# A tap in eight on GpSimd with partial sums in PSUM, and a reordered last pass, in an fp32 image kernel

## The reference, cut to what matters

```python
# layer 0: 512 channels in 256 groups of two
d = depthwise 3x3 conv, stride 2, padding 1            # (8, 256, 64, 64), 18 taps per output
labels = kmeans(d[0]);  gate = sigmoid(from a mixture fit on cluster means of d)
up = repeat(gate * d + d, 2, axis=1) * w_up
x = bilinear_up_x2(up) + x                             # (8, 512, 128, 128)
# layer 1: attention over 64 low cosine frequencies P (16384 x 64)
xP = einsum('bcn,nk->bck', x, P)                       # then products with Wq, Wk, Wv and norms
out = gamma * (WvxP @ (out / lamdv) + out_bias) + x
```

## Time and profile before

| what | value |
|---|---|
| time, median of 3 runs | 3655.98 us (3652.37 to 3658.43) |
| profiled execution: its own time, its span | 3661.4 us, 3659.6 us |
| TensorE busy in the span, mean granted clock | 85 %, 0.935 |
| VectorE busy | 81 % |
| ScalarE busy | 51 % |
| GpSimd busy | 17 % |
| first pass, start of the first and the last tap (L190) | 18.1 and 1354.6 us |
| second pass, start of the first and the last add | 1941.6 and 3650.4 us |

### The profile page before, as it was taken

The page is one execution under the profiler, slowest core; times in us unless marked ns, Lnnn a source line. Parts: engine busy times, 40 slices in busy tenths (PEclk is TensorE's granted clock), DMA queues, the critical chain, the costliest instruction groups (busy, mean ns, idle before and its releaser), DMA issues. The chain is left out here.

```text
span 3659.6 us, 66212 instructions
## 1 busy us (share of the span) xinstructions
PE 3128.9 (85%) x23398; PEld 2253.8 (62%) x23398; DVE 2957.6 (81%) x3454; ACT 1880.3 (51%) x4327; POOL 637.2 (17%) x325
## 2 busy tenths in 40 slices
PE   7998999999899958995867888889788888888876
PEld 3554545455454526652446877878687787878776
DVE  5999999999999982204556979888897988979877
ACT  4554555555455524241316565655656566565654
POOL 0000000000000000000003333333333333333333
PEclk9999999999999979597978999999999999999999
DMA  6665566556655525252035988988888898888997
GB/s 266 256 248 212 219 257 255 222 212 251 257 233 212 238 114 204 110 217 65 0 132 212 338 331 333 351 317 337 327 326 333 328 347 331 335 326 329 345 346 287
DMA packets 190940, 947.58 MB, mean 259 GB/s; under 512 B 13505, under 2 KB 13633, under 8 KB 170626
## 3 DMA queue, kind: packets, MB, share of 16 engines
q1 hardware_dynamic: 181378, 909.48, 64.3%
q0 software_dynamic: 9216, 33.56, 2.3%
HBM read 638.90 MB, written 301.99 MB: 257 GB/s over the span
## 5 line engine op out<-in xcount | busy, mean ns | idle before, releaser
L190 DVE SCALAR_TENSOR_TENSOR first_acc<-first_x,first_wd,first_acc 128x1024 f32<-128x1024 f32 (+1 forms) x1088 | 1297.9, 1272 | 58.0 <-ACT first_acc L215 45.2
L1290 PE MATMUL second_o<-second_right,second_left 128*128 128x128 f32 x8192 | 1101.0, 285 | 175.2 <-POOL second_left L1074 98.7
L1290 PEld LDWEIGHTS second_o<-second_right,second_left 128*128 128x128 f32 x8192 | 1016.8, 199 | 229.7 <-issue 217.9
L1534 DVE SCALAR_TENSOR_TENSOR second_x<-second_o,second_shift,second_x 128x512 f32<-128x512 f32 x1024 | 732.9, 737 | 233.1 <-PE second_o L1290 231.5
L1074 POOL TENSOR_TENSOR second_left<-second_mid_copy,second_coef_rep 64x1024 f32<-64x1024 f32 x256 | 602.5, 2353 | 1684.5 <-ACT second_mid_copy L1397 1677.4
L219 ACT ACTIVATE first_xT<-first_tp 128x512 f32<-128x512 f32 x1024 | 609.3, 598 | 536.1 <-PE first_tp L245 535.6
L245 PE MATMUL first_tp<-all_const,first_x 128*128 128x128 f32 x4096 | 680.5, 291 | 75.3 <-issue 40.8
L245 PEld LDWEIGHTS first_tp<-all_const,first_x 128*128 128x128 f32 x4096 | 442.3, 143 | 458.7 <-issue 446.3
L257 PE MATMUL first_freq<-first_xT,first_p 128*64 128x256 f32 x4096 | 669.2, 408 | 17.9 <-ACT first_xT L219 8.2
L1376 ACT ACTIVATE second_mid<-second_dd,all_inter 128x128 f32<-128x128 f32 x1024 | 327.1, 390 | 388.1 <-DVE second_mid L1515 384.9
L257 PEld LDWEIGHTS first_freq<-first_xT,first_p 128*64 128x64 f32 x4096 | 210.9, 136 | 194.7 <-issue 178.9
(11 more groups left out here) (233 smaller groups left out, 2005.5 us busy)
## 6 DMA issues: line engine op xcount, KB each, us to landing
second_x<-in_x SPq DMA_DIRECT2D x256, 1024.0 KB, 10.2
out<-second_x SPq DMA_DIRECT2D x256, 1024.0 KB, 6.4
first_x<-in_x SPq DMA_DIRECT2D x48, 4224.0 KB, 25.3
first_x<-in_x SPq DMA_DIRECT2D x16, 4096.0 KB, 14.9
...
downsampled<-first_acc POOLq DMA_DIRECT2D x64, 512.0 KB, 11.5
...
```

The lines of the kernel that those rows point to most:

```text
L190: nc.vector.scalar_tensor_tensor(out=acc[c][:, :, left:], in0=tap_window(xt[c], (s, dh, dw), OUT1), scalar=wd[:, t, k:k + 1], in1=acc[c][: ...
L1290: last = nc.tensor.matmul(ob[n][:, r, :], left[a][:, r, n, :], right[a][:, r, :], start=True, stop=True)
L1534: nc.vector.scalar_tensor_tensor(out=xt[i][:, n // S, n % S, rows, :], in0=ob[n][:, :, :], scalar=shift[:, n:n + 1], in1=xt[i][:, n // S, ...
```

## The change

In the first pass GpSimd takes over 17 taps on the lower half of chunk 3 (`POOL_CHUNK`): an eighth of VectorE's elements. [...] VectorE keeps its running sums in PSUM (`partial`), from tap 2 to tap 16; only its first tap reads `acc` and its last writes it. Chunks 0 and 1 stay as pairs of 1024 elements; in phase 2 it works on three halves of 512. To make room, the transposes have two PSUM buffers in place of four and the fold shares the banks of the sums. Chunk 3's first tap moves on ScalarE from quad 48 to quad 34, stores move to SyncE's queue ahead of each load, and loops hold eight images a turn.

In the last pass `turn_mid` of the next unit goes ahead of the unit's first product, `copy` ahead of both halves of `weight`, `scale_odd` ahead of the first add, `frequencies` behind the fourth, and loads and stores of the two halves `t` have semaphores of their own.

```diff
--- before.py
+++ after.py
-TAPS = [(s, dh, dw) for dw in (0, 1) for dh in (-1, 0, 1) for s in range(S)] + \
-       [(s, dh, -1) for dh in (-1, 0, 1) for s in range(S)]
+TAPS = [(s, dh, dw) for dw in (0, -1, 1) for dh in (-1, 0, 1) for s in range(S)]
 ROWS1 = 32
 CH1 = H // ROWS1
 TAPS_LEFT = len(TAPS) - 1
 OUT1 = ROWS1 // 2
 QUADS = S * ROWS1 // 4
 SLOTS = 4
+TP_BANKS = 2
+UNROLL1 = 4
+POOL_CHUNK = 3
+FIRST_TAPS = [0, QUADS, 2 * QUADS, 2 * QUADS + 2]
+STEPS = [TAPS_LEFT, TAPS_LEFT, 2 * TAPS_LEFT, 2 * TAPS_LEFT]
+
+
+def weight_of(s, dh, dw):
+
+    k = s * 9 + (dh + 1) * 3 + dw + 1
+    return slice(k, k + 1)
...
-        tp = [sc.ps(f"tp{i}", [P, 4, P]) for i in range(SLOTS)]
+        tp = [sc.ps(f"tp{i}", [P, 4, P]) for i in range(TP_BANKS)]
         freq_ps = [sc.ps(f"freq{t}", [P, 512]) for t in range(T)]
-        sum_ps = sc.ps("sum", [P, 512])
+        sum_ps = [bank[:, S * P:S * P + S * UV] for bank in freq_ps]
+        product = sc.sb("product", [P, OUT1 // 2, WD])
+        partial = [sc.ps(f"partial{i}", [P, OUT1, WD]) for i in range(2)]
         halves = sc.sb("halves", [P, S * P])
...
+                def store(i, c):
+
+                    sp.wait_ge(tapped[c], i * STEPS[c] + STEPS[c] + FREE)
+                    if c == POOL_CHUNK:
+                        sp.wait_ge(upper_tapped, i * TAPS_LEFT + TAPS_LEFT + FREE)
+                    sp.dma_start(xd.rearrange("b t g n -> (b t) g n")[i, :, c * OUT1 * WD:(c + 1) * OUT1 * WD],
+                                 acc[c][:, :, :].rearrange("g h w -> g (h w)")).then_inc(stored[c], 16)
+
+                start_free(sp, stored)
+                with sp.Fori(0, B * T - 1) as i:
                     for c in range(CH1):
-                        load(i, c)
+                        store(i, c)
...
+                start_free(pool, [tapped[POOL_CHUNK]])
+                c, rows = POOL_CHUNK, slice(OUT1 // 2, OUT1)
+                for i in range(B * T):
+                    done = i * STEPS[c] + FREE
+                    pool.wait_ge(x_in[c], i * 16 + 16)
+                    pool.wait_ge(started, i * CH1 + c + 1)
+                    for n, (s, dh, dw) in enumerate(TAPS[1:]):
+                        left = 1 if dw < 0 else 0
+
+                        if n > 0 or i > 0:
+                            pool.wait_ge(tapped[c], done + 2 * n)
+                        nc.gpsimd.tensor_scalar(product[:, :, left:],
+                                                tap_window(xt[c], (s, dh, dw), OUT1 // 2, OUT1 // 2),
+                                                wd[:, i % T, weight_of(s, dh, dw)], None, ALU.mult
+                                                ).then_inc(tapped[c], 1)
+                        pool.wait_ge(tapped[c], done + 2 * n + 1)
+                        nc.gpsimd.tensor_tensor(acc[c][:, rows, left:], acc[c][:, rows, left:], product[:, :, left:],
+                                                ALU.add).then_inc(tapped[c], 1)
...
+                def tap(t, c, n, rows, mine):
+
+                    s, dh, dw = TAPS[1 + n]
+                    left = 1 if dw < 0 else 0
+                    row0, count = rows.start, rows.stop - rows.start
+                    before = acc[c] if n == 0 else mine
+                    after = acc[c] if n == TAPS_LEFT - 1 else mine
+                    return nc.vector.scalar_tensor_tensor(
+                        out=after[:, rows, left:], in0=tap_window(xt[c], (s, dh, dw), count, row0),
+                        scalar=wd[:, t, weight_of(s, dh, dw)], in1=before[:, rows, left:],
+                        op0=ALU.mult, op1=ALU.add)
+
+                with dve.Fori(0, B // UNROLL1) as r:
+                    for n_image in range(UNROLL1 * T):
+                        t, i = n_image % T, r * UNROLL1 * T + n_image
+                        for n in range(TAPS_LEFT):
+                            for c in (0, 1):
+                                if n == 0:
+                                    dve.wait_ge(x_in[c], i * 16 + 16)
+                                    dve.wait_ge(started, i * CH1 + c + 1)
+                                    if c == 0:
+
+                                        dve.wait_ge(tapped[2], i * STEPS[2] + FREE)
                                     else:
 
+                                        dve.wait_ge(upper_tapped, i * TAPS_LEFT + FREE)
+                                else:
+
+                                    dve.wait_ge(tapped[c], i * STEPS[c] + n + FREE)
+                                tap(t, c, n, slice(0, OUT1), partial[c]).then_inc(tapped[c], 1)
+                        c, half = 2, OUT1 // 2
+                        for n in range(TAPS_LEFT):
+                            for h in range(2):
+                                if n == 0 and h == 0:
+                                    dve.wait_ge(x_in[c], i * 16 + 16)
+                                    dve.wait_ge(started, i * CH1 + c + 1)
+
+                                    dve.wait_ge(tapped[0], i * STEPS[0] + STEPS[0] + FREE)
+                                elif n > 0:
+
+                                    dve.wait_ge(tapped[c], i * STEPS[c] + 2 * n + h - 1 + FREE)
+                                tap(t, c, n, slice(h * half, (h + 1) * half), partial[0]).then_inc(tapped[c], 1)
+                            if n == 0:
+                                dve.wait_ge(x_in[POOL_CHUNK], i * 16 + 16)
+                                dve.wait_ge(started, i * CH1 + POOL_CHUNK + 1)
+
+                                dve.wait_ge(tapped[1], i * STEPS[1] + STEPS[1] + FREE)
+                            else:
+
+                                dve.wait_ge(upper_tapped, i * TAPS_LEFT + n + FREE)
+                            tap(t, POOL_CHUNK, n, slice(0, half), partial[1]).then_inc(upper_tapped, 1)
...
-                            slot, c = q % SLOTS, q // QUADS
-                            if q % QUADS == 0:
+                            slot = q % SLOTS
+                            if q in FIRST_TAPS:
+                                c = FIRST_TAPS.index(q)
                                 act.wait_ge(x_in[c], i * 16 + 16)
 
-                                act.wait_ge(stored[c], i + FREE)
+                                act.wait_ge(stored[c], i * 16 + FREE)
                                 nc.scalar.activation(acc[c][:, :, :], tap_window(xt[c], TAPS[0], OUT1), ACT.Copy,
...
-                            pe.wait_ge(copied[slot], i * (quads // SLOTS) + q // SLOTS + FREE)
+                            before = (q - TP_BANKS) % SLOTS
+                            pe.wait_ge(copied[before], i * (quads // SLOTS) + (q - TP_BANKS) // SLOTS + 1 + FREE)
...
+                    for t in range(T):
+                        if u % 2 == 1:
+                            store(b, m, t)
+                        if u % 2 == 1 and (more or m + AHEAD < CH2):
+                            load_image(b, m + AHEAD, t)
...
                 def step(b, u, more):
+                    if more or u < UNITS - 1:
+                        turn_mid(b, u + 1)
                     for n in range(BANKS):
                         multiply(b, u, n)
-                        if more or u < UNITS - 1:
-                            if n == 0:
-                                turn_mid(b, u + 1)
-                            elif n == 1:
-                                turn_zt(b, u + 1)
+                        if n == 1 and (more or u < UNITS - 1):
+                            turn_zt(b, u + 1)
                     if more:
                         stage(b + 1, u)
...
-                    ahead = u % 2 == 1 and (more or m + 2 < CH2)
-                    if ahead:
-                        weight(b, m + 2, 0)
                     if more or u < UNITS - 1:
                         copy(b, u + 1)
-                    if ahead:
+                    if u % 2 == 1 and (more or m + 2 < CH2):
+                        weight(b, m + 2, 0)
                         weight(b, m + 2, 1)
...
-                    if n == 0 and u % 2 == 0:
-                        dve.wait_ge(x_in[i], (b * (CH2 // XBUF) + m // XBUF) * T * 16 + T * 16)
+                    if n % S == 0 and u % 2 == 0:
+                        dve.wait_ge(x_in[i][n // S], (b * (CH2 // XBUF) + m // XBUF) * 16 + 16)
...
+                    if more or u < UNITS - 1:
+                        if u == UNITS - 1:
+                            take_coef(b, 1)
+                        scale_odd(b, u + 1)
                     for n in range(BANKS):
                         add(b, u, n)
-                        if n == 0 and (more or u < UNITS - 1):
-                            if u == UNITS - 1:
-                                take_coef(b, 1)
-                            scale_odd(b, u + 1)
-                        if n == 1 and u % 2 == 0 and (more or m + 1 < CH2):
-                            frequencies(b, m + 1)
                         if n == 2 and u % 2 == 0 and (more or m + 1 < CH2):
                             interpolate(b, m + 1)
```

(2 more changed lines are left out.)

101 lines of the change are left out of this document (36 added, 65 removed).

## The result

| | before | changed |
|---|---|---|
| median of 5 runs | 3657.06 us | **3680.87 us** (3670.57 to 3683.67) |
| ratio | | 1.006, 95% interval 1.0042 to 1.0077 |
| profiled execution, span, granted clock | 3659.6 us, 0.935 | 3681.9 us, 0.926 |
| first pass, start of VectorE's last tap | 1354.6 us | 1315.6 us |
| last pass, first to last add | 1941.6 to 3650.4: 1708.8 us | 1898.6 to 3674.8: 1776.2 us |

The kernel became 24 us slower; forecast were 156 faster. The span's +22 us are two changes of opposite sign: the last pass starts 43 us earlier and takes 67 us longer.

The account below looks back on a forecast made before the run. VectorE's work was taken to bound the first pass, with TensorE close behind, and a chain through several engines the last. Profiled 3661.4 - 35 - 100 - 21 = 3505, said as 3500 us against the runs' median; range 3390 to 3600.

Parts of the forecast that it names:

- First pass, -35 us: First pass: image period falls from 82.1 to 79.9 us, over 16 images -35 us.
- A: First pass: PSUM is dear, each VectorE tap takes 0.06 us more, +5 in place of -35, 3540 us; chance 0.12.
- C: First pass: reading and writing the same PSUM bank halves VectorE's rate in the running sums, 4425 us; chance 0.08.
- D: First pass: GpSimd late, its chain takes 82 us, the pass gains nothing, 3535 us; chance 0.06.
- my 0.8 us: First pass: price of one GpSimd product of 512, within a tap of 2.2 us and 37 us an image.
- Last pass, -121 us: Last pass: seven batches with stage gain 100 us, the last batch 21 (205 to 184).
- 11.1 us against 12.68: Last pass: the pair's new chain, from bank 0 of an odd unit, takes 11.1 us where it took 12.68.
- Two banks at 0.9 each: Last pass: first link of the pair's new chain, two TensorE banks at 0.9 us each.
- GpSimd at 2.35: Last pass: link of the pair's new chain behind the copy, GpSimd's half of left at 2.35 us.
- A "new wait" of 1.1, hidden: Last pass: TensorE waits 1.1 us for interpolation, making 10.9 a pair, hidden under 11.1 by little.
- My allowance of 0.4 for DMA: Last pass: a pair taken at 11.5 us, above the chain's 11.1, with DMA needing 11.8 a pair.
- rival B: Last pass: DMA decides earlier, at 345 GB/s a batch's floor is 205 us; 3529 us, or 3560 with waits; chance 0.14.

Follow-up runs that it names:

- e1: Changed first pass with the last pass of the kernel before: 3610.06 us, 0.9881 of the kernel before.
- e11: e1 with VectorE's running sums left in SBUF (acc) from first tap to last: 4056.30 us, 446 us slower than e1.
- e8: Changed kernel with four more TensorE products behind bank 3 of each even unit, ahead of the turn, their result overwritten: 3636.84 us.
- e7: e3 with interpolate behind the second add in place of the third: 3440.32 us, 0.9399 of the kernel before.
- e3: Changed kernel with the first half of the weighting back ahead of the copy: 3486.92 us, 0.9542 of the kernel before.
- e9: e3 with frequencies back behind bank 1, ahead of interpolation: 3603.03 us, 116 us slower than e3.
- e4: Changed kernel with frequencies back behind bank 1, ahead of interpolation: 3809.97 us, 1.0422 of the kernel before.
- e10: e3 with the turn of the middle rows back behind bank 0: 3551.02 us, 64 us slower than e3.
- e2: Changed kernel with the turn of the middle rows (turn_mid) back behind bank 0: 3608.53 us, 0.9883 of the kernel before.

## Why the prediction was wrong, point by point

**First pass, -35 us: right.** The period is 79.9 us, as forecast, with 81.9 and 77.5 in turn; alone it gave 45 us (e1). The cause is the forecast one too, a wait for chunk 3 in every other image, at 3.3 us where my sum had 4.8. Taps at 1.19 and 0.66 held, so rivals A and C did not occur; nor did D, whose 18 us for a single load had no row.

GpSimd's product was mis-sized: 1612 ns against my 0.8 us. A tap takes about 1.61 + 1.28 = 2.9 us, 49 us an image, and not 37. It stayed hidden, but not with the room I gave it: in 7 images the store of chunk 3, and with it the next load, waits for GpSimd, 4.7 us at most. In the image looked at (its store waits until 203 us) ScalarE did not wait for the load that followed.

What I undervalued is why the sums are in PSUM: I named the collision and gave it no price; it is 446 us (e11). The page "SBUF — State Buffer" of the Trainium skill, section "Who interferes with whom", says that a VectorE instruction with two SBUF inputs contends with a GpSimd instruction that reads SBUF. The 3599 against 1654 ns agrees. The page "VectorE: DVE Perf Modes" of the Trainium skill, section on the errata of TRN2, gives VectorE a higher fixed cost from PSUM than from SBUF. That does not show here: 0.66 us a tap of 512 in PSUM (the changed kernel), and 0.66 a tap of 504 in SBUF (e11).

**Last pass, -121 us: wrong, it is +67.** The step that failed is the sum of the pair's new chain, "11.1 us against 12.68", together with the sentence that TensorE's wait of 1.1 us is "hidden under 11.1". In the last batch the chain itself was the right one. Its links were priced from rows of an order in which they are undisturbed:

- *Two banks at 0.9 each.* I had seen the two waits, one for the interpolation and one for GpSimd, and asked only whether their length was covered. The banks behind them ran at a granted clock of 0.52: 3.4 us for the two banks in place of 1.8. My sum for the first pass held 0.4 us an image for the clock, and that for the last pass nothing. e8 shows 1.6 us a pair, and 44 us over the kernel from filling one of the two waits. Over the last pass TensorE's instructions, equal in number, took 1473 us in place of 1440.
- *GpSimd at 2.35.* I wrote that `frequencies` no longer meets GpSimd, and did not ask what meets it instead. The copy now starts GpSimd when the interpolation is due: 1842 ns for L1581 at the median. In the last batch `frequencies` meets it all the same (1878 ns in the mean), and the product beside both takes 3.0 us.
- *A "new wait" of 1.1, hidden.* It was there before, 107 us in 92 times, about 1.2 each. It is now 247.4 us in 114 times, 2.2 each, and in the batches with `stage` it is what TensorE waits for: 31 us a batch where it was 12, against 15 less behind GpSimd. In all TensorE stands 38 us of such a batch where it stood 33, and its instructions take 187 where they took 183: that is the 9 us.
- For a pair of the last batch, 11.1 + 1.6 + 0.65 = 13.35 against 13.17 measured. That batch takes 206 us where I forecast 184. The others take 225 where I forecast 216 - 14 = 202; no such sum was made for their pairs. My allowance of 0.4 for DMA was not needed, and rival B did not occur: e7 moves 402 GB/s in its last batch.

**A wrong reading of the chain of before.** I took the weightings between interpolation and copy for what the change removes. In e3 they stand there still, the stretch is as long as before, and the pair takes 10.8 us. The gain comes from the other stretch, bank 0 to interpolation: `frequencies` out of it (116 to 129 us, e9 and e4), and the early turn (64 us, e10). The two are not a sum: from e1 to e3 it is 123 us, and without the early turn only 59 (e10). Even by my own price of 11.1 the late weighting is no gain over 10.8; I never priced the change without it.

**The three moves do not add.** The early turn gains 64 us with the weighting split and loses 72 with it in one piece. The late weighting costs 57 us with the turn behind bank 0 and 194 with it ahead. The early turn only gets `mid_t` ready; if ScalarE is then busy for 4.8 us, nothing behind it starts earlier, and TensorE's wait for GpSimd (196 us in e2) becomes one for the interpolation (247). That the lower clock comes with the pair of moves is seen in the traces (1.00 in the banks of e3, 0.52 in the changed kernel).

TensorE's time tells how the loss divides. From the first to the last add, by the windows view, with 11992 to 11996 of its instructions in each:

| | stretch | TensorE busy | standing | granted clock |
|---|---|---|---|---|
| before | 1709 us | 1440 | 269 | 0.96 |
| changed | 1776 us | 1473 | 303 | 0.93 |
| e3 | 1589 us | 1388 | 201 | 0.98 |

So of the 187 us between the changed kernel and e3, 85 are the same instructions at a lower clock, and 102 are time in which TensorE stands. Its wait for the interpolation fell by 102 us (240.7 to 138.8 in these stretches). How much of that standing is GpSimd's collision and how much a longer chain is open.

**The rivals.** None of mine held the result. The only one on the slower side was in the first pass, and the last pass, where three quarters of the gain were to come from, had none of that sign. My range, to 3600, had there only smaller gains. (The chance of "faster" does not add up either: all but C and half of the rest is 0.905, not 0.89.)

The best version is e7: changed first pass, early turn, early `scale_odd`, late `frequencies`, half of the weighting ahead of the copy and `interpolate` behind the second add, 3440.32 us, 6.0 % less than before.
